# One TensorE row half for each of two heads in the first attention, gathers of four experts packed into three

## Chip, core and metric

The kernel runs on one core of a Trainium2 chip. The metric is the device time of one launch in microseconds. The core has TensorE (matmuls into PSUM), VectorE, ScalarE, GpSimd and SyncE (SP, which here only issues DMAs), and 16 DMA engines.

## What is computed

Two sequences of 1024 tokens with 256 features go through four blocks: a causal attention with rotary embedding (16 heads of 16 features), a layer norm with a ternary-weight projection, a causal attention with 16 heads of 128 features, and a mixture of 64 experts. Cut to the parts that the change touches:

```python
# first attention: x (2, 1024, 256), 16 heads of 16
q, k, v = proj(Wq), proj(Wk), proj(Wv)
q, k = rope(q), rope(k)
scores = where(causal, q @ k.T / 4, lowest)
attn = softmax(scores) @ v
y = attn @ Wo.T
# experts: 64, top 6 of 64 within the best 3 of 8 groups, capacity 96 rows each
slot = flat * C + min(pos, C - 1)
buf = zeros(E * C, H).at[slot].set(x[tok])
out = (silu(buf @ Wg.T) * (buf @ Wu.T)) @ Wd.T      # for each expert
y = sum(out[slot] * topk_w) + shared_expert(x)
```

All of it is float32. The kernel writes queries and keys of the attentions as sums of a high and a low f16 part.

## The kernel before

The stages follow each other with a barrier between them: norm, the projections of the first attention (`l0_qkv`), `l0_attention`, its output projection, the second layer, `norm`, `l1_attention` for each sequence, the router, `experts` and `combine`.

**`l0_attention`.** 32 heads (16 in each of two sequences) run one after the other; a pair of heads shares the value product. For each head GpSimd's `fetch` copies the parts of q and k into `qh` and `kh` (128 tokens by 8 blocks by 128 columns; 64 columns carry the four products of high and low parts, one more carries the maximum, the rest are zero). SP turns them with a DMA transpose (`turn`, lines 583 and 588). TensorE computes for each block of 128 queries the scores against all earlier keys (`max_scores`, "rows", line 624, the causal mask added by line 627), VectorE reduces them to the negated maximum, written into a column of `qh` (line 737), and SP turns `qh` once more (line 600). With that, TensorE computes for each block of keys the scores of all later queries less their maximum ("columns", line 682, mask 687), and ScalarE takes the exp into `pT` (line 725). The score banks are two deep for rows (`S1`) and two for columns (`ST`), each up to 1024 wide. TensorE alternates a column step and the row step that lies `EARLY` = 6 steps ahead. Within a pair's 16 steps `SESSIONS` puts ten rounds of value matmuls of the pair before (line 645: four matmuls into four column groups, f32) in four stretches; then ScalarE evacuates zT (line 714), TensorE turns it (658), VectorE divides (744, 751).

In the same block the weights of the second attention are split into f16 parts, 24 jobs: SP loads one (`w_load`, line 822; 16 jobs of 384 KB, then 8 of 256 KB), GpSimd splits it (`w_split`, lines 805, 811, 813), SP stores it (`w_store`, 827). There are two buffers for input and two for parts. GpSimd also issues 24 zero-fills of `choice_rows` (line 571), one a head. GpSimd's order in head m is `fetch(m)`, `fetch_values(m - 2)`, `w_split(m - 4)`, zero-fill; SP's is the turn of `qh` with the maxima of m, `turn(m + 2)`, `w_store(m - 3)`, `w_load(m - 1)`. Semaphores count: `w_in` for what is fetched, `t_in` and `tm_in` for what is turned, `m_ready` for maxima, `st_ready` and `s1_ready` for scores, `e_ready` for exps.

**`experts`.** The router leaves for each expert the list of its 96 tokens in `src` and of their destinations in `dst` (lines 1677 to 1685). GpSimd gathers the 96 rows of each expert (line 1742), 16 experts ahead; TensorE turns them, two experts at a time (`turn_pair`, 1779), VectorE copies them (1904). The expert's matmuls are `gu` (1793) and `down` (1802); ScalarE copies the result (1879) and GpSimd scatters it (1751). SP loads the experts' weights, 528 KB each, 16 ahead: the first 10 in the router, six more at the start of this block (lines 1722 to 1724), the others as buffers come free. At the start TensorE also finishes the shared expert's last four tiles (1412) and, between the first and the second expert, turns the weights of overflowing tokens (1823); VectorE and ScalarE take part (`overflow`, `turned_overflow`). `combine` then loads the rows of every token and adds them up.

## Time and profile before

| | |
|---|---|
| three runs | 1574.81, 1579.88, 1579.84 us; median 1579.84 |
| profiled execution | 1579.99 us, its span 1578.3 us |
| mean granted TensorE clock | 0.941 |
| first attention | about 96 to 398 us of the span |
| experts and combining | from about 1355 us to the end |

The span reaches from the first to the last instruction of the profiled execution; what lies around it makes up the rest of its time. Busy times are those of the profiler's records. A granted clock of 1.00 is 2.4 GHz, 0.50 is 1.2 GHz. "idle before <-X" names what ended an engine's idle time.

### The profile page before, as it was taken

The page shows a single profiled execution, that of the slowest core. Times are in us where ns is not written, and L with a number is a line of the kernel's source. Part 1 is how long each engine was busy: PE and PEld are TensorE (multiplying, and loading weights), DVE is VectorE, ACT ScalarE, POOL GpSimd, SP SyncE. Part 2 cuts the span into 40 slices and gives each one's busy share as a digit, 9 for nine tenths or more (in the row PEclk, how much of TensorE's full clock was granted, in tenths as well). Part 3 has the DMA queues.
Part 4 walks back from the last instruction along what each step waited for, and adds up shares of the span by engine and source line. Part 5 has one row for each costly group of instructions (what it writes and reads, how often), then busy time and mean ns, then how long its engine had stood idle before and what let it go on. Part 6 is the DMA issues. An engine that isn't in the chain of part 4 may idle for free. (4 is left out here: it accounts for less than half of the span.)

```text
span 1578.3 us, 36418 instructions
## 1 busy us (share of the span) xinstructions
PE 1407.0 (89%) x12869; PEld 985.8 (62%) x12869; DVE 1050.9 (67%) x2197; ACT 813.1 (52%) x1676; POOL 375.3 (24%) x796
## 2 busy tenths in 40 slices
PE   3848999998669999999979999999998798699977
PEld 2414555454555777777767677777777645599953
DVE  4766777775766888888841888888882368522229
ACT  1215656556216777777730787777781115333330
POOL 0344656430020111111120111111101000477730
PEclk9968999999869999999999999999999789799985
DMA  3027999972023755556540566556652340599948
GB/s 100 1 59 158 243 250 240 212 170 54 1 77 77 139 134 137 133 136 139 136 91 1 112 138 140 135 133 140 140 122 44 106 118 0 141 290 300 283 131 291
DMA packets 463402, 215.08 MB, mean 136 GB/s; under 512 B 412083, under 2 KB 434449, under 8 KB 463073
## 3 DMA queue, kind: packets, MB, share of 16 engines
q1 hardware_dynamic: 448992, 175.09, 46.9%
q0 software_dynamic: 12000, 36.90, 7.9%
q10 hardware_dynamic: 2336, 2.16, 0.4%
q8 instruction: 39, 0.64, 0.2%
q14 instruction: 35, 0.28, 0.1%
HBM read 81.97 MB, written 31.52 MB: 72 GB/s over the span
## 5 line engine op out<-in xcount | busy, mean ns | idle before, releaser
L1055 PE MATMUL bank<-a_pt,v_part 128*128 128x128 f16 x3456 | 234.2, 219 | 14.9 <-DMA a_pt<-a_ph 9.5
L737 DVE TENSOR_REDUCE a_qh<-bank 128x1 f16<-128x1024 f32 (+7 forms) x256 | 182.3, 755 | 86.5 <-PE bank L627 84.9
L1118 ACT ACTIVATE a_ph<-a_p,a_rinv 128x1024 f16<-128x1024 f32 (+7 forms) x256 | 198.6, 777 | 79.0 <-POOL a_rinv L997 76.0
L1055 PEld LDWEIGHTS bank<-a_pt,v_part 128*128 128x128 f16 x3456 | 207.7, 98 | 48.4 <-DMA a_pt<-a_ph 7.8
L1126 DVE TENSOR_REDUCE a_negm<-bank 128x1 f32<-128x1024 f32 (+7 forms) x256 | 191.8, 750 | 55.9 <-PE bank L1039 55.7
L1034 PE MATMUL bank<-a_k,a_q 128*128 128x512 f16 (+3 forms) x1152 | 228.6, 326 | 0.2
L725 ACT ACTIVATE a_p<-bank 128x1024 f32<-128x1024 f32 (+7 forms) x256 | 158.0, 650 | 129.8 <-PE bank L682 113.8
L1160 DVE SCALAR_TENSOR_TENSOR a_ph<-a_p,a_rinv,a_ph 128x1024 f16<-128x1024 f32 (+7 forms) x256 | 206.9, 808 | 1.7 <-ACT a_ph L1118 1.7
L1107 ACT ACTIVATE a_p<-bank,a_negm 128x1024 f32<-128x1024 f32 (+7 forms) x256 | 189.5, 740 | 21.6 <-DVE a_negm L1126 21.5
L997 POOL TENSOR_TENSOR a_rinv<-a_rinv,p_scale 128x1 f32<-128x1 f32 x256 | 49.0, 191 | 615.4 <-DVE a_rinv L1139 615.2
L906 PE MATMUL bank<-x_part,wsplit 128*128 128x512 f16 x768 | 187.3, 381 | 4.0 <-PEq L188 1.8
L624 PE MATMUL bank<-a_k,a_q 128*128 128x512 f16 (+3 forms) x384 | 109.5, 342 | 33.8 <-DMA a_k<-a_kh 19.4
L1034 PEld LDWEIGHTS bank<-a_k,a_q 128*128 128x128 f16 x1152 | 99.4, 98 | 60.6 <-ACT a_p L1107 1.2
L682 PE MATMUL bank<-a_qm,a_k 128*128 128x512 f16 (+3 forms) x384 | 113.0, 333 | 6.6 <-ACT a_p L725 5.2
L906 PEld LDWEIGHTS bank<-x_part,wsplit 128*128 128x128 f16 x768 | 70.1, 98 | 72.2 <-issue 5.6
L1742 POOL DMA_INDIRECT x_rows<-token_rows,src x64 | 63.1, 986 | 172.6 <-issue 170.2
L1793 PE MATMUL bank<-x_T,wgu 128*88 128x96 f32 x1024 | 96.4, 248 | 0.7 <-issue 0.7
L915 PE MATMUL bank<-wsplit,x_part 128*128 128x128 f16 x1536 | 95.9, 219 | 0.8 <-DVE a_k L941 0.5
L1793 PEld LDWEIGHTS bank<-x_T,wgu 128*88 128x88 f32 x1024 | 92.9, 158 | 4.5 <-issue 1.0
L915 PEld LDWEIGHTS bank<-wsplit,x_part 128*128 128x128 f16 x1536 | 88.2, 98 | 5.7 <-DVE a_k L941 2.1
L1911 DVE TENSOR_TENSOR x_h<-bank,x_sg 88x192 f32<-88x192 f32 x64 | 22.6, 354 | 94.8 <-ACT x_sg L1870 94.8
L1188 PE MATMUL bank<-wo_part,z_part 128*128 128x256 f16 x768 | 84.2, 273 | 1.7 <-PEq L966 1.7
(206 smaller groups left out, 2246.4 us busy)
## 6 DMA issues: line engine op xcount, KB each, us to landing
wgu<-in_wgu SPq DMA_DIRECT2D x64, 352.0 KB
choice_rows<-zero POOLq DMA_DIRECT2D x24, 512.0 KB, 5.2
c_rows<-choice_rows SPq DMA_DIRECT2D x16, 768.0 KB, 11.5
wsplit<-w_parts POOLq DMA_DIRECT2D x30, 384.0 KB, 3.9
wd<-in_wd SPq DMA_DIRECT2D x64, 176.0 KB
pw_in<-in_wqkv SPq DMA_DIRECT2D x16, 384.0 KB, 5.3
w_parts<-pw_part SPq DMA_DIRECT2D x16, 384.0 KB, 2.9
a_pt<-a_ph SPq DMA_TRANSPOSE x256, 3.0
```

Of the source, the lines that this page charges most:

```text
L682: ins = pe.matmul(ST[k % 2][:, c4 * 512:c4 * 512 + w_], kT[s][:, kb, :], queries[:, kb * P + c4 * 512:kb * P + c4 * 512 + w_], start=True, ...
L725: act.activation(pT[s][:, off[kb]:off[kb + 1]], ST[k % 2][:, 0:(BT - kb) * P], ACT.Exp).then_inc(e_ready, 1)
L737: dve.tensor_reduce(qh[s][:, i, MC:MC + 1], s1_place(t), AX.X, ALU.max, negate=True).then_inc(m_ready, 1)
L906: ins = pe.matmul(G_ps[k % 2], w[:, a, c_, (k // 2) * P:(k // 2 + 1) * P], g.xs[x_][:, c_, b * S + (k % 2) * 512:b * S + (k % 2 + 1) * 512 ...
L915: ins = pe.matmul(G_ps[k % 2][:, j * P:(j + 1) * P], g.xs[x_][:, c_, t * P:(t + 1) * P], w[:, a, c_, 2 * P:3 * P], start=(c_ == 0 and (a, ...
L1034: ins = eng.matmul(ps[:, c4 * 512:c4 * 512 + w_], qT[par][a][:, i * P:(i + 1) * P], kT[par][k_][:, c4 * 512:c4 * 512 + w_], start=(a, k_) ...
L1055: ins = eng.matmul(Z_ps[:, cols], g.vs[par][v_][:, k, :], turned[slot][:, a * blocks[j] + k, :], start=(k == 0 and (v_, a) == PARTS[0]), s ...
L1107: eng.activation(probs[j % NBUF][:, 0:w_], S_ps[j % 4][:, 0:w_], ACT.Exp, bias=negm[:, par, j:j + 1], accum_out=rsum[:, par, j:j + 1]).the ...
L1118: eng.activation(parts[slot][:, 0:w_], probs[slot][:, 0:w_], ACT.Copy, scale=rinv[:, p_, jj:jj + 1]).then_inc(p_hi, 1)
L1126: eng.tensor_reduce(negm[:, par, j:j + 1], S_ps[j % 4][:, 0:blocks[j] * P], AX.X, ALU.max, negate=True).then_inc(m_ready, 1)
L1160: eng.scalar_tensor_tensor(parts[slot][:, w_:2 * w_], probs[slot][:, 0:w_], rinv[:, p_, jj:jj + 1], parts[slot][:, 0:w_], ALU.mult, ALU.su ...
L1793: ins = pe.matmul(b_[:, m * C:(m + 1) * C], g.wgu[s][:, c_, m * MH:(m + 1) * MH], xeT[(s // 2) % 2][:, s % 2, c_, :], start=(c_ == 0), sto ...
```

## The change

In the first attention the two heads of a pair are packed into one set of tiles: head 0 in the first 64 rows of the turned tiles, head 1 in the other 64. Each head has 48 columns for three products (high by high, low by high, high by low; the product of the low parts is left out) and one for the maximum. Rows and columns are cut into pieces of at most 512 columns, 24 rows and 24 columns for a pair (`ROWS`, `COLS`, alternating between the heads); the banks are three deep on each side. In each step the row piece, which belongs to the other head than the column piece, is issued first, then the column piece, then the masks in halves of 64 rows (`swapped` holds identity and mask rolled by 64 rows). The maxima of blocks with two pieces are joined from `half`. The queries are copied a second time into `qhm` for the turn with the maxima, the keys are turned twice (`kT`, `kTb`). Value rounds come in five stretches of two. SP and GpSimd do one iteration for each pair, with two weight jobs in it.

In the experts three gathers of 128 rows bring four experts' 384 rows; `src` is packed for it by small matmuls with `c_shift` at the router's end; `turn_group` turns them in six transposes, and VectorE copies them in one instruction. SP's loads for experts 10 to 15 wait for the first turn. The overflow's turn is moved behind the experts' loop.

```diff
+                sp.dma_start(swapf[:, :, :], g.t["c_swapped"]).then_inc(s_c, 16)
...
-    MC = 4 * DH0
+    HP = P // 2
+    MC = 3 * DH0
-    w_in = [g.sem(f"a0_w{i}") for i in range(2)]
-    t_in = [g.sem(f"a0_turned{i}") for i in range(2)]
-    tm_in = [g.sem(f"a0_turned_max{i}") for i in range(2)]
-    v_in = g.sem("a0_v_in")
-    FETCH = 5
+    t_in, tb_in, tm_in = [g.sem(f"a0_turned{n}") for n in ("", "_keys", "_max")]
+    w_in, wm_in, v_in, c_ready = [g.sem(f"a0_{n}") for n in ("w", "w_max", "v_in", "max_column")]
+    FETCH = 4
     ROUNDS = 2 * CH + 2
-    SESSIONS = {1: (0, 1, 2), 3: (3, 4), 7: (5, 6), 9: (7, 8, 9)}
-    ZT_STEP, TURN_STEP, Z_STEP = 11, 13, 15
-    ORDER = (0, 7, 1, 6, 2, 5, 3, 4)
-    EARLY = 6
+    SESSIONS = {1: (0, 1), 5: (2, 3), 9: (4, 5), 13: (6, 7), 17: (8, 9)}
+    ZT_STEP, TURN_STEP, Z_STEP = 18, 20, 22
+    ROWS = ((6, 1), (6, 0), (4, 1), (5, 0), (5, 1), (7, 1), (2, 0), (7, 0), (0, 0), (3, 0), (1, 0), (4, 0))
+    COLS = ((0, 0), (7, 0), (0, 1), (6, 0), (1, 0), (5, 0), (2, 0), (3, 1), (3, 0), (2, 1), (4, 0), (1, 1))
+    NS = 2 * NC_
+    NB_ = 3
+    EARLY = 13
...
+        qhm = [g.sb(f"a0_qhm{i}", [P, BT, P], F16, c) for i in range(2)]
+        half = g.sb("a0_half", [P, 2, 2, BT // 2, 2], F32, c)
+        ST = [g.bank[0][:, 0, :], g.bank[0][:, 1, :], g.bank[1][:, 0, :]]
+        S1 = [g.bank[2][:, 0, :], g.bank[2][:, 1, :], g.bank[1][:, 1, :]]
...
+                def queries(dst, m, done):
+                    q = dst[m % 2].rearrange("p t (h c) -> p h t c", h=2)
+                    src = g.qk[:, 2 * m:2 * m + 2, :, 0, :]
+                    pool.tensor_copy(q[:, :, :, 0:2 * DH0], src).then_inc(done, 1)
+                    pool.tensor_copy(q[:, :, :, 2 * DH0:MC], src[:, :, :, 0:DH0]).then_inc(done, 1)
                 def fetch(m):
                     if m >= 2:
+                        pool.wait_ge(t_in, 32 * (m - 1))
+                        pool.wait_ge(tb_in, 16 * (m - 1))
+                    queries(qh, m, w_in)
+                    k = kh[m % 2].rearrange("p t (h c) -> p h t c", h=2)
+                    src = g.qk[:, 2 * m:2 * m + 2, :, 1, :]
+                    pool.tensor_copy(k[:, :, :, 0:DH0], src[:, :, :, 0:DH0]).then_inc(w_in, 1)
+                    pool.tensor_copy(k[:, :, :, DH0:MC], src).then_inc(w_in, 1)
+                def fetch_again(m):
+                    if m >= 2:
+                        pool.wait_ge(tm_in, 16 * (m - 1))
+                    queries(qhm, m, wm_in)
...
+                for m in range(2, NP):
                     fetch(m)
+                    fetch_again(m)
                     fetch_values(m - 2)
+                    for q in (2 * m - 4, 2 * m - 3):
+                        if q < WJOBS:
+                            w_split(pool, q)
+                        if q < ZD:
+                            pool.dma_start(zv[q], g.zero[:, :]).then_inc(g.s_zero, 16)
+                fetch_values(NP - 2)
+                fetch_values(NP - 1)
...
+                def turned(dst, src, m, done):
+                    sp.dma_start_transpose(dst[m % 2].rearrange("p (t n) -> p t n", n=P),
+                                           src[m % 2].rearrange("p t d -> p (t d)")).then_inc(done, 16)
                 def turn(m):
+                    sp.wait_ge(w_in, FETCH * (m + 1))
+                    if m >= 1:
+                        sp.wait_ge(t_in, 32 * m)
                     if m >= 2:
+                        sp.wait_ge(s1_ready, (m - 1) * NS)
+                    turned(kT, kh, m, t_in)
+                    turned(qT, qh, m, t_in)
+                def turn_keys(m):
+                    if m >= 1:
+                        sp.wait_ge(tb_in, 16 * m)
+                    if m >= 2:
+                        sp.wait_ge(st_ready, (m - 1) * NS)
+                    turned(kTb, kh, m, tb_in)
                 turn(0)
                 turn(1)
+                turn_keys(0)
                 w_load(sp, 0)
                 w_load(sp, 1)
+                for m in range(NP):
+                    sp.wait_ge(c_ready, 2 * m + 2)
+                    if m >= 1:
+                        sp.wait_ge(tm_in, 16 * m)
                     if m >= 2:
+                        sp.wait_ge(st_ready, (m - 1) * NS)
+                    turned(qmT, qhm, m, tm_in)
+                    if m + 2 < NP:
                         turn(m + 2)
+                    for q in (2 * m - 2, 2 * m - 1):
+                        if 0 <= q < WJOBS:
+                            w_store(sp, q)
+                    for q in (2 * m, 2 * m + 1):
+                        if 2 <= q < WJOBS:
+                            w_load(sp, q)
+                    if m + 1 < NP:
+                        turn_keys(m + 1)
...
+                def scores(col, row):
+                    if row is not None:
+                        t, m, par, at_start = row
+                        hr, i, k0, nr_ = row_piece(t)
+                        if t == 0:
+                            pe.wait_ge(t_in, m * 32 + 32)
+                        if not (at_start and t < NB_):
+                            pe.wait_ge(m_ready, m * NS + (t - NB_ + 1))
+                        at = slice(hr * HP, (hr + 1) * HP)
+                        rs = S1[t % NB_]
+                        r_diag = k0 + nr_ == i + 1
+                        ri = pe.matmul(rs[:, 0:nr_ * P], qT[par][at, i * P:(i + 1) * P],
+                                       kT[par][at, k0 * P:(k0 + nr_) * P], start=True, stop=not r_diag)
+                    if col is not None:
+                        k, m, par, at_start = col
+                        hc, kb, q0, nc_ = col_piece(k)
+                        if k == 0:
+                            pe.wait_ge(tm_in, m * 16 + 16)
+                            pe.wait_ge(tb_in, m * 16 + 16)
+                        if not (at_start and k < NB_):
+                            pe.wait_ge(e_ready, m * NS + (k - NB_ + 1))
+                        at = slice(hc * HP, (hc + 1) * HP)
+                        cs = ST[k % NB_]
+                        c_diag = q0 == kb
+                        ci = pe.matmul(cs[:, 0:nc_ * P], kTb[par][at, kb * P:(kb + 1) * P],
+                                       qmT[par][at, q0 * P:(q0 + nc_) * P], start=True, stop=not c_diag)
+                    for x in range(2):
+                        if row is not None and r_diag:
+                            ident, mask = halves(hr)[x]
+                            ri = pe.matmul(rs[:, (nr_ - 1) * P + x * HP:nr_ * P], ident, mask[:, x * HP:P],
+                                           start=False, stop=x == 1)
+                        if col is not None and c_diag:
+                            ident, mask = halves(hc)[x]
+                            ci = pe.matmul(cs[:, x * HP:(x + 1) * HP], mask, ident[:, x * HP:(x + 1) * HP],
+                                           start=False, stop=x == 1)
+                    if row is not None:
+                        ri.then_inc(s1_ready, 1)
+                    if col is not None:
+                        ci.then_inc(st_ready, 1)
...
+                    if i >= BT // 2:
+                        dve.tensor_reduce(half[:, par, h, i - BT // 2, k0 // 4:k0 // 4 + 1], S1[t % NB_][:, 0:n_ * P],
+                                          AX.X, ALU.max).then_inc(m_ready, 1)
+                    else:
+                        dve.tensor_reduce(qhm[par][:, i, h * HP + MC:h * HP + MC + 1], S1[t % NB_][:, 0:n_ * P],
+                                          AX.X, ALU.max, negate=True).then_inc(m_ready, 1)
+                    if t >= NS - 2:
+                        dve.wait_ge(m_ready, m * NS + (t + 1))
+                        dst = qhm[par][:, BT // 2:BT, h * HP + MC:h * HP + MC + 1].rearrange("p t o -> p (t o)")
+                        dve.tensor_reduce(dst, half[:, par, h, :, :], AX.X, ALU.max, negate=True).then_inc(c_ready, 1)
...
+            sp.wait_ge(s_t, 1)
...
+            def gather(n, j):
+                pool.indirect_dma_start(out=rows[n % NR][:, j, :], out_offset=None, in_=g.xrows,
+                                        in_offset=bass.IndirectOffsetOnAxis(ap=g.src[:, j, n:n + 1], axis=0),
+                                        bounds_check=T - 1, oob_is_err=False).then_inc(s_row[n % NR], 16)
+            for n in range(LOOK):
+                for j in range(NPK):
+                    gather(n, j)
...
+            def turn_group(n, q):
+                pe.wait_ge(s_row[q], n * (NPK * 16 // NR) + (NPK * 16 - NPK * 16 // NR * q))
+                if not (isinstance(n, int) and n == 0):
+                    pe.wait_ge(s_tc, n)
+                for c_ in range(DC):
+                    for j in range(NPK):
+                        ins = pe.transpose(g.bank[0][:, c_, j * P:(j + 1) * P],
+                                           rows[q][:, j, c_ * P:(c_ + 1) * P], g.identf[:, :])
...
+            pe.wait_ge(s_sf, 1)
+            for j in range(NPK):
+                for q, at in PACK[j]:
+                    ins = pe.matmul(packed[:, j, :], g.shift[:, at:at + P],
+                                    srcf.rearrange("p (e q) -> p e q", q=XG)[:, :, q],
+                                    start=(q == PACK[j][0][0]), stop=(q == PACK[j][-1][0]))
+            ins.then_inc(s_ix, 1)
...
-            walk(act, lambda p_num, s: None, silu, out_rows, turned_overflow)
+            walk(act, lambda p_num, s: None, silu, out_rows)
+            turned_overflow()
...
-            walk(dve, turned, product, lambda i, e, s: None, overflow)
+            walk(dve, turned, product, lambda i, e, s: None)
+            overflow()
```

## Rows read from the trace of the kernel before

**Rows 1.** Busy time by window, first attention: engines, granted clock, DMA share, GB/s.
```profile
160.00:200.00 40.00, 37.96 (x391) 20.36 (x393) 28.41 (x51) 24.18 (x40) 26.05 (x49) 1.00 1.03 246
...
320.00:360.00 40.00, 37.69 (x376) 20.33 (x368) 28.45 (x50) 24.61 (x41) 13.43 (x37) 1.00 0.73 160
```

**Rows 2.** Timeline of ScalarE: first and fourteenth evacuation of zT (start, duration).
```profile
151.13 0.60 ACT L714 ACTIVATE a_zt<-bank 128x512 f32<-128x512 f32 x1
...
373.14 0.60 ACT L714 ACTIVATE a_zt<-bank 128x512 f32<-128x512 f32 x1
```

**Rows 3.** Timeline of TensorE around a stretch of value matmuls.
```profile
242.84 0.22 PE L687 MATMUL bank<-identb,maskb 128*128 128x128 bf16 x1
242.89 0.33 PE L682 MATMUL bank<-a_qm,a_k 128*128 128x384 f16 x1
...
243.91 1.06 PE L645 MATMUL bank<-a_p,a_vh 128*17 128x256 f32 x16
244.90 0.39 PE L682 MATMUL bank<-a_qm,a_k 128*128 128x512 f16 x1
```

**Rows 4.** Busy time by window, start and middle of the experts.
```profile
1362.00:1366.00 4.00, 0.77 (x4) 0.34 (x2) 0.76 (x2) 0.00 (x0) 3.05 (x4) 0.97 1.05 276
1366.00:1370.00 4.00, 2.63 (x15) 2.37 (x16) 2.36 (x3) 0.00 (x0) 3.39 (x3) 0.50 0.81 247
...
1380.00:1420.00 40.00, 40.00 (x377) 36.16 (x376) 10.47 (x25) 12.03 (x34) 30.25 (x33) 1.00 0.98 289
```

**Rows 5.** Timeline of the experts' start.
```profile
1355.74 7.03 PE L1412 MATMUL bank<-sd,shared_h_late 128*128 128x256 f32 x24 [2.98 <-DVE x L1924]
...
1359.49 0.96 POOL L1742 DMA_INDIRECT x_rows<-token_rows,src  x1 [0.30 <-issue]
...
1366.67 0.90 PE L1779 MATMUL bank<-identf,x_rows 96*128 96x96 f32 x4 [3.90 <-DMA x_rows<-token_rows,src]
...
1374.25 1.49 PE L1793 MATMUL bank<-x_T,wgu 128*88 128x96 f32 x16
```

**Rows 6.** Groups by shape, first attention: count, busy us, mean ns.
```profile
L737 DVE TENSOR_REDUCE a_qh<-bank 128x1 f16<-128x512 f32 x32 | 21.9, 683 | 0.0
...
L813 POOL TENSOR_TENSOR pw_part<-pw_in,pw_part 128x512 f16<-128x512 f32 x8 | 9.2, 1151 | 0.7
...
L737 DVE TENSOR_REDUCE a_qh<-bank 128x1 f16<-128x128 f32 x32 | 9.1, 283 | 0.0
...
L811 POOL CAST pw_part<-pw_in 128x512 f16<-128x512 f32 x8 | 4.9, 614 | 23.0 <-DMA pw_in<-in_wo 23.0
```

**Rows 7.** Timeline of SP's issues and of GpSimd, one head.
```profile
245.00 0.61 POOL L805 TENSOR_TENSOR pw_in<-pw_in,pw_scale 128x256 f32<-128x256 f32 x1 [3.40 <-DMA pw_in<-in_wqkv]
...
246.16 1.33 SPq L588 DMA_TRANSPOSE a_k<-a_kh  x1
...
247.54 0.57 SPq L827 DMA_DIRECT2D w_parts<-pw_part  x1
...
248.16 0.59 POOL L571 DMA_DIRECT2D choice_rows<-zero  x1
248.16 0.46 SPq L822 DMA_DIRECT2D pw_in<-in_wqkv  x1
248.75 0.41 POOL L546 COPY a_qh<-qk_parts 128x256 f16<-128x256 f16 x1
```

**Rows 8.** DMA issues of 200 to 300 us: count, KB, median us to landing.
```profile
pw_in<-in_wqkv SPq DMA_DIRECT2D x7, 384.0 KB, 5.5
pw_in<-in_wo SPq DMA_DIRECT2D x5, 256.0 KB, 4.3
...
a_q<-a_qh SPq DMA_TRANSPOSE x12, 3.4
```

**Rows 9.** Timeline of the first attention's first score matmul and last exps.
```profile
105.82 0.61 PE L624 MATMUL bank<-a_k,a_q 128*128 128x512 f16 x1 [17.21 <-DMA a_k<-a_kh]
...
389.93 1.19 ACT L725 ACTIVATE a_p<-bank 128x640 f32<-128x640 f32 x2 [0.21 <-PE bank L682]
```

More of the change, by code:

```diff
@@ L696, in pair @@
-                def pair(which, p, n0, s0):
-                    for h in range(2):
-                        for k in range(BT):
-                            step(which, p, n0 + h, s0 + h, h, k)
-                            if which != "first":
-                                for r in SESSIONS.get(h * BT + k, ()):
-                                    value_round(pe, r, p - 1, n0 - 2, (s0 + 2) % 4)
+                    scores(None, (t, 1, 1, False))
+                def pair(which, p, par):
+                    for k in range(NS):
+                        ahead, t = s1_step(k)
+                        row = None if skipped(which, ahead) else (t, p + ahead, (par + ahead) % 2, False)
+                        scores((k, p, par, which == "first"), row)
+                        if k == TURN_STEP and which != "first":
+                            turn_z(pe, p - 1)
+                        if which != "first":
+                            for r in SESSIONS.get(k, ()):
+                                value_round(pe, r, p - 1, 1 - par)
@@ L1366 @@
 XG = 4
+NPK = XG * C // P
+PACK = [[(q, C + j * P - q * C) for q in range(XG) if q * C < (j + 1) * P and (q + 1) * C > j * P]
+        for j in range(NPK)]
+LOOK = 3
 XP = 10
```

319 lines of the change are left out of this document (124 added, 195 removed).

## The prediction

> **What bounds the kernel now.** I read the stretches of the first attention first (the table by window), because most of the diff is there. TensorE is busy 38 of 40 us, VectorE 28, ScalarE 24, GpSimd 13 to 26, and the DMA engines' share falls from 1.03 to 0.73 [rows 1]. Then the evacuations of zT, one for each pair of heads: 13 pitches in 222 us, 17.1 us a pair [rows 2]. The pitch is the same where the DMA share is 1.03 and where it is 0.73, so neither the DMA engines nor the splitting of the second attention's weights sets it: it is TensorE, with its waits for the two-deep score banks. One 128-column matmul with its weight load follows the other after 0.05 us, 16 value matmuls (two rounds) take 1.06 us from the first start to the last end, of which 0.2 are the last one's own pipeline, so 0.85, and 0.14 us more pass until the next score matmul [rows 3]. By hand, a pair of heads is 22,528 f16 columns (9.4 us at 2.4 GHz), 80 value matmuls (4.3), the turn of zT (0.6), so 14.3 of the 17.1 us. In the experts TensorE is busy all 40 of 40 us, with the DMA engines at 0.98 [rows 4]; ahead of them it waits 3.90 us for gathered rows [rows 5].
>
> **The first attention's new work on TensorE.** Each score piece now contracts over 64 rows, one head in each half of the array, and a row piece of one head is issued beside a column piece of the other. Counting both streams step by step and taking the longer of each step, I get 13,824 columns, 5.8 us a pair; 112 matmuls with weight loads at 0.05 us [rows 3] are 5.9. If the halves don't overlap, the 24,576 columns are 10.2 us. No row of before shows two row halves. The nearest shows column groups: 16 value matmuls of 256 f32 columns, which one after the other would take some 3 us, in 0.85 [rows 3]. I take the overlap. Then TensorE needs 5.9 + 4.3 + 0.6 + 5 gaps of 0.15 = 11.6 us.
> The Trainium skill (TensorE: Matmul & The Clock Gate, Part 3: Packing small matmuls) says that matmuls on distinct row groups run together; by it the 5.9 stands, and no row here shows it. A rule against the change is in TensorEngine Tiling (Array Packing), Tiling Modes: going from one tiling mode to another drains the engine. The 0.14 us gap behind a value stretch agrees; with ten such changes a pair instead of eight it is worth 0.3 us, within the gaps counted.
>
> **VectorE and ScalarE.** VectorE is busy 28.4/40 x 17.1 = 12.1 us a pair. The same 9,216 columns are now reduced in 24 pieces instead of 16; the fixed part of a reduction is 0.15 us (283 ns at 128 columns, 683 at 512 [rows 6]), half of it overlapped, so 8 x 0.07 = 0.6, and two small reductions over `half`, each behind a wait for its own predecessor, 0.5: 13.2 us. Five value stretches of 0.85 us leave it dry some 0.3 us each (three banks of at most 512 columns hold 1.4 to 1.7 us of its work, and the next piece comes 1.7 to 1.9 us later): 14.7 us a pair. The bounds are 13.2 and 17.1. ScalarE has 10.3 us and 8 more starts, about 11; it doesn't bind.
>
> **The loop that takes over: weights, GpSimd, SP.** This is the step on which I differ from the sum above. Before, a head's iteration of SP is qm turn, turn(m + 2), one store, one load, and GpSimd's is fetch(m), one split. A load goes out two iterations before the turn that its split delays, so the loop load, split, fetch, two turns, store spans two heads: 5.5 + 3.2 + 0.6 + 1.5 + 2.6 + 0.6 = 14 us in 17.1. After, an iteration is a pair: SP issues turn(m + 2), stores 2m - 2 and 2m - 1, then loads 2m and 2m + 1; GpSimd does fetch(m + 2) first and then splits 2m and 2m + 1. turn(m + 3) waits for w_in, thus for fetch(m + 3), which stands behind both splits of 2m and 2m + 1 on GpSimd; and the next two loads stand behind turn(m + 3) and both stores on SP. So everything is in one chain once a pair:
> zero-fill DMA 0.6, fetch with two copies of 512 and two of 256 elements 2.0 (256 take 0.41), two transposes issued 2.6, two stores 1.15, load to landing 5.5, split 3.15, zero-fill 0.6, split 3.15 [rows 7, 8] = **18.8 us**. For the eight `wo` jobs (four pairs) the landing is 4.3 [rows 8] and a split 1.15 + 0.61, with a gap 1.8 [rows 6]: 15.1 us.
> The nearest rows for each link are those of before, with the same SP and GpSimd operations; unknown are only the 512-element copies (between 0.41 and 0.82) and the landing beside two stores and a second load (5.2 to 6.5). That gives 18.2 to 20.5 for the loop.
> It is above 14.7, so after the slack is gone (turn(m) is some 7 us ahead at first) pairs go at the loop's pace, and TensorE waits about 4 us a pair for `a0_turned` at step 11, the first row piece of the pair after next.
>
> **The attention's timeline.** First score matmul at 105.8 as now [rows 9]. 37 row pieces come before the first column, at VectorE's 0.6 us: columns from 128, and c_ready for pair 1 eleven steps later, at 134. From there to fetch(4): qm and two turns 3.9, stores 1.15, landing 5.5, splits and zero-fills 7.5, fetch 2.0: 154. Six loops of 18.8 and four of 15.1 bring fetch(14) to 327.3, and its turn lands 4.7 later (one issue, and 3.4 to landing [rows 8]), at 332, step 11 of pair 12. Then two pairs at 14.7, 13 steps with columns alone 7.0, the last pair 12.5 (TensorE: 12,288 columns in one stream 5.1, value matmuls 4.3, turn 0.6, gaps and waits 2.5): 381. Before, the last exp ends at 391.1 [rows 9]. **-10.2 us.** The final ten value rounds are as they were.
>
> **The experts.** The gathers are 48 of 128 rows instead of 64 of 96, the turns six of 128 columns instead of eight of 96, the same 768 columns; GpSimd and VectorE aren't the bound there. So the pace (377 matmuls in 40 us [rows 4], 22 an expert, 2.34 us) stays: 0 (bounds -3 and +3). The start changes. Now TensorE finishes the late shared rows at 1362.8, gets its rows at 1366.67 (the fourth gather, issued at 1359.49, lands 7.1 us later beside 3.2 MB of weights), and with the turned overflow in between the second expert's matmuls start at 1374.25 [rows 5]. After, three gathers suffice and SP's 12 weight loads wait for the first turn; I take the landing at 1362.8 or earlier (between 1360.5 and 1365.3). Turn 0.7, a copy of 768 columns 1.0, first expert 1.5, waits 0.3, packing at the router's end 0.6 later (one VectorE copy behind 12 small matmuls): the second expert at 1366.9 + 0.6 = 1367.5. **-6.7 us** (bounds -4 and -8). The overflow's turn now lies where TensorE and VectorE wait for the combining rows, over 10 us, and needs 6: hidden. The 12 loads are 8 us late; the first of these experts is wanted some 20 us later: nothing.
> The load of `c_swapped` ahead of x costs one issue, **+0.5**. The extra casts and `c_shift` lie behind x and the norm: 0.
> Sum: 1579.99 (the profiled execution, 1578.3 of span and 1.7 around it; the median of three is 1579.84) - 10.2 - 6.7 + 0.5 = **1564 us**.
>
> **Rivals.**
> A, the loop does not bind, because loads, fetch or issue are quicker together than I add up or more work is ahead than I count. For it: the loop of today has 3 us to spare and never shows in the pitch. Against: the order of the two programs. Attention then 128 + 13 + 13.5 x 14.7 + 19.5 = 358, -33: **1541 us**. Chance 0.14.
> B, the change doesn't do what it says: the row halves run one after the other. Then a pair is 17.9 us of TensorE; hidden under 18.8 six times, +2.8 in four pairs and +3.2 in two, some 2 at both ends, +20: **1584 us**. Chance 0.12, for only column groups are shown.
> C, the loop is longer, 20 to 20.5, its landing slowed by two stores and a second load: +10 to +15, **1577 us**. For it: stores and loads of this stage have never stood this close together. Chance 0.08.
> D, the clock. After 3.9 us of waiting for the rows of the experts the granted clock was 0.50, the 1.2 GHz level, against 0.97 in the stretch ahead [rows 4]; the wait of 4 us a pair at step 11 is as long. At 1.2 GHz a pair is 2 x 10.2 + 1 = 21 us. A clock low for half of the pair gives 17.6 us and stays hidden under 18.8; low for over about 70% of it, it is the new bound, and low throughout +2.4 in six pairs and +6 in four: **1603 us**, slower. Chance 0.05.
> The forecast itself 0.61, with its own range 1556 to 1573.
>
> **Numbers.** 0.5% is 7.9 us, about what a measurement here can tell. Faster: 0.53 of the forecast's 0.61, all of A, 0.01 of C = 0.68. Slower: B 0.04, C 0.02, D 0.05 = 0.11. The same: 0.21. The range reaches from A to B, 1540 to 1586.
>
> **What would show it.** Right: evacuations of zT 18 to 20 us apart for six pairs, then 15, then less than 15; the first row piece of each pair waiting for the DMA of `a0_k` or `a0_q`; SP waiting in the turn for GpSimd's copies; GpSimd waiting for pw_in. Overlap: row and column matmuls starting within 0.05 us with a step no longer than its wider piece. Wrong if the pitch is 14 to 15 from pair 2 on (A), if steps with two 512-column pieces last over 0.45 us at full clock (B), or if the stretches show a clock near 0.5 (D). In the experts the first turn should come at once behind the shared rows.

## The result and the profile after

The kernel after takes 1561.28 us (median of four runs, 1559.74 to 1562.85), the kernel before 1579.86 beside it: ratio 0.988 with a 95% interval of 0.9856 to 0.9904. The profiled execution took 1561.47 us, its span is 1559.4, 18.9 less than before.

First the pace of the first attention, by the page's most plain mark, ScalarE's evacuation of zT once a pair (line 787). Its starts are 148.49, 163.63, 179.04, 199.09, 214.59, 233.54, 251.92, 268.34, 283.49, then 14.9 to 15.0 apart up to 328.25, and 342.75, 356.84, 369.87, 377.24. Before it was 17.0 from pair to pair (once 17.7, the last two less) and ended at 395.40: the attention is 18.2 us shorter. Busy time by window (as [rows 1]):

```profile
160.00:200.00 40.00, 32.34 (x460) 17.05 (x457) 30.82 (x74) 25.54 (x60) 24.45 (x35) 0.91 0.74 200
...
320.00:360.00 40.00, 34.54 (x519) 18.00 (x511) 30.77 (x79) 30.10 (x72) 3.96 (x9) 1.00 0.38 75
```

TensorE has 32 us of work in 40 where it had 38; no engine is busy all the time. TensorE's timeline around a stretch of value matmuls (as [rows 3]; 729 is a row piece, 744 a column piece, 696 the values):

```profile
172.05 0.39 PE L729 MATMUL bank<-a_k,a_q 64*128 64x512 f16 x1
172.13 0.38 PE L744 MATMUL bank<-a_qm,a_kb 64*128 64x512 f16 x1
...
172.50 1.06 PE L696 MATMUL bank<-a_p,a_vh 128*17 128x256 f32 x16
173.50 0.33 PE L729 MATMUL bank<-a_k,a_q 64*128 64x384 f16 x1
173.50 0.33 PE L744 MATMUL bank<-a_qm,a_kb 64*128 64x384 f16 x1
```

Row and column piece of these steps start 0 to 0.08 us apart: the two halves of the array work at once. A step of two 512-column pieces takes 0.22 us up to its masks (171.53 to 171.75). What sets the pitch stands on SP's and GpSimd's timelines (as [rows 7]):

```profile
149.81 0.62 POOL L585 COPY a_qh<-qk_parts 128x512 f16<-128x512 f16 x1
...
151.67 1.23 SPq L633 DMA_TRANSPOSE a_k<-a_kh  x1
152.96 1.33 SPq L633 DMA_TRANSPOSE a_q<-a_qh  x1
154.34 1.07 SPq L909 DMA_DIRECT2D w_parts<-pw_part  x2
155.45 1.78 SPq L904 DMA_DIRECT2D pw_in<-in_wqkv  x2
...
160.59 0.61 POOL L887 TENSOR_TENSOR pw_in<-pw_in,pw_scale 128x256 f32<-128x256 f32 x1 [7.70 <-DMA pw_in<-in_wqkv]
...
168.14 0.62 POOL L585 COPY a_qh<-qk_parts 128x512 f16<-128x512 f16 x1
...
170.01 1.23 SPq L633 DMA_TRANSPOSE a_k<-a_kh  x1
```

From turn to turn 18.34 us: two turns 2.67, stores 1.11, load to first split 5.14, two splits and two zero-fills 7.55, copies 1.87. The turn of pair 4 (pairs are numbered from 0) starts at 151.67, that of pair 10 at 259.33: six loops of 17.9 us on average. The other links are the same in all six to 0.02 us; what varies is the landing, 4.49 to 5.14 us, 4.75 in the mean. TensorE gets the end of it, and its clock too (its timeline, and windows of 2 us):

```profile
192.36 0.50 PE L729 MATMUL bank<-a_k,a_q 64*128 64x384 f16 x1 [3.07 <-DMA a_q<-a_qh]
```

```profile
188.00:190.00 2.00, 1.29 (x22) 0.46 (x17) 1.70 (x5) 1.11 (x3) 0.98 (x3) 1.00 0.57 105
190.00:192.00 2.00, 0.00 (x0) 0.00 (x0) 0.10 (x1) 0.00 (x0) 0.00 (x0) 0.84 1.07 246
192.00:194.00 2.00, 1.64 (x18) 0.98 (x21) 0.83 (x2) 0.89 (x2) 0.00 (x0) 0.50 1.09 324
194.00:196.00 2.00, 2.00 (x23) 0.67 (x24) 0.92 (x2) 0.68 (x2) 0.00 (x0) 0.50 0.94 332
196.00:198.00 2.00, 2.00 (x24) 0.98 (x24) 1.67 (x4) 1.61 (x4) 1.84 (x3) 0.50 1.19 235
198.00:200.00 2.00, 1.52 (x28) 0.93 (x21) 1.22 (x4) 1.20 (x5) 1.98 (x3) 0.95 0.33 73
```

Behind the wait of 3.07 us the granted clock is 0.50, the 1.2 GHz level, for almost 7 us. That makes this pitch 20.05 us, but the next is 15.50 and the two together are again two loops: the slow clock is hidden behind the loop.

The experts' start (as [rows 5]); the first turn of gathered rows (line 1885) now comes straight behind the late shared rows (1502), and the clock of 1352 to 1356 is 1.00 where it was 0.50 behind the old wait:

```profile
1344.13 7.60 PE L1502 MATMUL bank<-sd,shared_h_late 128*128 128x256 f32 x24 [1.52 <-DVE x L2029]
1351.57 0.82 PE L1885 MATMUL bank<-identf,x_rows 128*128 128x128 f32 x6
1353.48 2.85 PE L1899 MATMUL bank<-x_T,wgu 128*88 128x96 f32 x32 [1.10 <-DVE x L2029]
```

Where the 18.9 us come from: attention -18.2; the blocks up to the second attention another -1.9; the second attention, in which nothing was changed, gives back 7.0; the experts' start, from the router's copy of `dst` (1354.02 before, 1340.81 after) to the second expert's first matmul (1374.25 and 1354.85), -6.2; the rest is +0.3, and rounding.

### The profile page after: what moved, and what is told of

Same layout as the page of the kernel before. It is cut to its first block and busy times, and to the rows that moved or that the text cites. A ratio compares the mean times of both kernels' runs of the same rounds, so it can differ in the third digit from the quotient of the medians.

```text
span 1559.4 us, 37733 instructions
## 1 busy us (share of the span) xinstructions
PE 1373.0 (88%) x13361; PEld 969.1 (62%) x13361; DVE 1061.9 (68%) x2343; ACT 821.2 (53%) x1804; POOL 354.4 (23%) x698
## 5 line engine op out<-in xcount | busy, mean ns | idle before, releaser
L1116 PE MATMUL bank<-a_k,a_q 128*128 128x512 f16 (+3 forms) x1152 | 228.7, 326 | 0.2
L797 ACT ACTIVATE a_p<-bank 128x512 f32<-128x512 f32 (+3 forms) x384 | 166.3, 492 | 103.4 <-PE bank L753 84.8
L812 DVE TENSOR_REDUCE a_half<-bank 128x1 f32<-128x512 f32 (+3 forms) x256 | 137.4, 583 | 38.7 <-PE bank L749 36.2
L729 PE MATMUL bank<-a_k,a_q 64*128 64x512 f16 (+3 forms) x384 | 117.8, 360 | 50.2 <-DMA a_q<-a_qh 26.7
L744 PE MATMUL bank<-a_qm,a_kb 64*128 64x512 f16 (+3 forms) x384 | 109.4, 343 | 1.8 <-ACT a_p L797 1.6
L729 PEld LDWEIGHTS bank<-a_k,a_q 64*128 64x128 f16 x384 | 34.5, 96 | 101.3 <-DVE a_half L812 44.4
L1849 POOL DMA_INDIRECT x_rows<-token_rows,src x48 | 49.1, 1024 | 169.2 <-POOLq L1591 154.9
```

What stands on the lines that cost most here:

```text
L729: ri = pe.matmul(rs[:, 0:nr_ * P], qT[par][at, i * P:(i + 1) * P], kT[par][at, k0 * P:(k0 + nr_) * P], start=True, stop=not r_diag)
L797: act.activation(pT[2 * par + h][:, at:at + n_ * P], ST[k % NB_][:, 0:n_ * P], ACT.Exp).then_inc(e_ready, 1)
L812: dve.tensor_reduce(half[:, par, h, i - BT // 2, k0 // 4:k0 // 4 + 1], S1[t % NB_][:, 0:n_ * P], AX.X, ALU.max).then_inc(m_ready, 1)
L1116: ins = eng.matmul(ps[:, c4 * 512:c4 * 512 + w_], qT[par][a][:, i * P:(i + 1) * P], kT[par][k_][:, c4 * 512:c4 * 512 + w_], start=(a, k_) ...
```

## The experiments

Ten kernels ran. Times are medians, the ratio is to the kernel before.

**1. Stores and loads ahead of the turns.** SP's order alone.

```diff
                     turned(qmT, qhm, m, tm_in)
-                    if m + 2 < NP:
-                        turn(m + 2)
                     for q in (2 * m - 2, 2 * m - 1):
                         if 0 <= q < WJOBS:
                             w_store(sp, q)
                     for q in (2 * m, 2 * m + 1):
                         if 2 <= q < WJOBS:
                             w_load(sp, q)
+                    if m + 2 < NP:
+                        turn(m + 2)
```

> Changed against the kernel after: SP issues the two stores and the two loads of a pair ahead of turn(m + 2), not behind it. My theory: the loop of 17.9 us a pair in the kernel after is the once-a-pair chain fetch, two turns, stores, loads, landing, two splits. With this order fetch and turn hang beside it, and stores 1.15, landing 5.0, splits and a zero-fill 6.9 make 13.1 to 13.6 us, under the 14.9 us that pairs take at the end of the attention, where no weights are moved. So all pitches of zT come to 14.9 to 15.5 us, the wait of TensorE for the row turn (26.7 us in seven places) goes, and the kernel takes about 1547 us, 14 less than the 1561 of the kernel after. Rival (the longer pitch of the pairs with weight jobs comes from TensorE, VectorE or the transfers being slower beside 0.75 of DMA share): the pitch stays at 17 to 18 us and the time at 1561 +- 2.

1547.05 us, ratio 0.978 [0.9751, 0.9809], 14.2 us below the kernel after; the last evacuation of zT comes 14.3 us earlier, at 362.98. Every pitch from the second to the tenth pair is 14.88 to 15.15 us, no wait of TensorE is over 1 us from 140 to 345, and no window of 2 us there has a clock below 0.9. SP's and GpSimd's timelines:

```profile
206.96 1.05 SPq L909 DMA_DIRECT2D w_parts<-pw_part  x2
208.05 1.71 SPq L904 DMA_DIRECT2D pw_in<-in_wqkv  x2
209.87 2.08 SPq L633 DMA_TRANSPOSE a_k<-a_kh  x1
...
214.45 0.61 POOL L887 TENSOR_TENSOR pw_in<-pw_in,pw_scale 128x256 f32<-128x256 f32 x1 [4.27 <-DMA pw_in<-in_wqkv]
...
221.41 0.59 POOL L626 DMA_DIRECT2D choice_rows<-zero  x1
...
221.93 1.05 SPq L909 DMA_DIRECT2D w_parts<-pw_part  x2
```

GpSimd still waits for the load, but 4.27 us, not 7.70: turns and copies now lie beside the landing. The chain was the bound, and the order of two issues made it. The rival is out: the DMA share rises to 0.93 in 160 to 200 and the pitch falls. What is left of the chain is longer than the 13.1 to 13.6 us expected, since the load lands later beside the turns: stores 1.09, load to first split 6.40, splits and a fill 6.96 make 14.5 us, only 0.4 under the pitch.

**2. Row and column piece in the same half.**

```diff
-    EARLY = 13
+    EARLY = 12
```

> Changed against the kernel after: EARLY 12 instead of 13, so that in each step the row piece and the column piece belong to the same head, and so lie in the same half of the rows of TensorE; all else is as it was. My theory (pieces in different halves run together and are worth 4 us of TensorE a pair): matmuls of a step start one behind the other, the pitch at the end of the attention, without weight jobs, goes from 14.9 to 17.5 to 18.5 us, and the pairs with weight jobs from 17.9 to 18 to 19; the kernel takes 1575 to 1585 us. Rival (VectorE sets the 14.9 us, and the overlap of the halves is worth little in time): pitches 14.9 to 15.5 at the end, the time 1561 +- 3.

1582.67 us, ratio 1.0027 [1.0012, 1.0043]. The pitch is 17.33 to 17.38 us from the second pair to the eleventh, with weight jobs and without: TensorE binds everywhere. It is busy 36.8 us in each 40 (180 to 340), 15.9 a pair. The loop of the turns still takes 18.0 us on average (154.06 to 262.03, six loops); the pitch doesn't show it, since the turns start some way ahead. TensorE's timeline:

```profile
337.07 0.39 PE L729 MATMUL bank<-a_k,a_q 64*128 64x512 f16 x1
337.30 0.38 PE L744 MATMUL bank<-a_qm,a_kb 64*128 64x512 f16 x1
```

0.23 us from row to column where the kernel after has 0 to 0.08; a step of two 512-column pieces takes 0.45 us instead of 0.22. The overlap is worth 2.4 us of pitch and 21 us of the whole; without it the change gains nothing. (The edit also shortens the lead of the rows by one step; that was not tried by itself.)

**3. Both zero-fills ahead of both splits.**

```diff
                     for q in (2 * m - 4, 2 * m - 3):
-                        if q < WJOBS:
-                            w_split(pool, q)
                         if q < ZD:
                             pool.dma_start(zv[q], g.zero[:, :]).then_inc(g.s_zero, 16)
+                    for q in (2 * m - 4, 2 * m - 3):
+                        if q < WJOBS:
+                            w_split(pool, q)
```

> Changed against the kernel after: GpSimd issues a pair's two zero-fills ahead of its two splits instead of one behind each, where it waits for the load anyway. My theory (a single chain once a pair through GpSimd and SP): 2 x 0.6 us leave the chain, the loop goes from 17.9 to 16.7 us in six pairs and from 14.6 to some 14.6 (there TensorE and VectorE bind), the kernel takes about 1554 us. Rival (the chain is not what binds, or the landing only fills the place of what leaves it): 1561 +- 2 and pitches of 17.9.

1601.72 us, ratio 1.0148 [1.0128, 1.0167]: 40 us slower than the kernel after, where I expected 7 less. Both theories miss. The loop is 21.2 us:

```profile
173.41 1.23 SPq L634 DMA_TRANSPOSE a_k<-a_kh  x1
174.70 1.34 SPq L634 DMA_TRANSPOSE a_q<-a_qh  x1
176.09 3.33 SPq L910 DMA_DIRECT2D w_parts<-pw_part  x2
179.47 2.59 SPq L905 DMA_DIRECT2D pw_in<-in_wqkv  x2
```

```profile
174.57 1.13 POOL L624 DMA_DIRECT2D choice_rows<-zero  x2
186.36 0.61 POOL L888 TENSOR_TENSOR pw_in<-pw_in,pw_scale 128x256 f32<-128x256 f32 x1 [10.67 <-DMA pw_in<-in_wqkv]
```

The fills' issue did leave the chain (1.2 us), but their transfers, 1 MB, now start 1.5 us ahead of SP's stores. The stores take 3.33 us to issue, not 1.07, the loads 2.59, not 1.78, and land in 6.6 us instead of 4.9 (medians of 200 to 260). From turn to first split it is 12.95 us where it was 8.92. In the kernel after a fill lands 2.9 us after its issue, before the next stores go out; here it takes 5.7 and is still under way beside them. TensorE waits 3.9 to 5.3 us in each of seven pairs, and the clock falls to 0.50 with each. In the prediction's sum a fill was its 0.6 us on GpSimd and no more. Experiments 5 and 6 ask what it is.

**4. The experts' part alone** (everything but the first attention as after; the attention as before).

> The experts' part of the change alone: everything as in the kernel after, but the first attention as it was before. My theory: the experts' part is worth 6 us, all at the start of the experts, and the first attention of the kernel after the rest, less what the granted clock takes back in the second attention: the kernel takes about 1574 us, and in the second attention the clock does not drop in the last heads (nothing in it has changed). Rivals: the clock's drop there comes with any of this change's parts or at random (then 1574 to 1581 with the drop in it); the gain of 6 us belongs to the earlier arrival at the experts, not to the packing (then 1580).

1575.56 us, ratio 0.9969 [0.9953, 0.9986]. The experts start as after: 17.5 us from the packing to the second turn (17.2 in the kernel after), first turn at once behind the late shared rows. So the 6 us belong to the experts' edits and not to the earlier arrival. The total shows only 3.4, since the unchanged second attention is 2.4 us longer by its clock: my expectation that the clock would not drop is wrong, and its rival (1574 to 1581, with the drop) holds.

**5. Zero-fills behind the loop.**

```diff
-                        if q < ZD:
-                            pool.dma_start(zv[q], g.zero[:, :]).then_inc(g.s_zero, 16)
                 fetch_values(NP - 2)
                 fetch_values(NP - 1)
+                for q in range(ZD):
+                    pool.dma_start(zv[q], g.zero[:, :]).then_inc(g.s_zero, 16)
```

> Changed against the kernel after: GpSimd issues the 24 zero-fills behind its last fetch of the first attention, not in its loop. What is disputed since the kernel with both fills ahead of the splits took 21.4 us a pair where the kernel after takes 17.9: my sum counts a fill as its 0.6 us of issue on GpSimd. Theory 1 (a fill costs its issue alone, the 21.4 has another cause): 1.2 us leave the loop, 16.7 us a pair, some 1554 us. Theory 2 (its 512 KB of transfer stand ahead of SP's stores and loads as well): the loop falls below the 14.9 us that TensorE and VectorE want, pitches of 15 to 15.5, and the kernel takes 1547 to 1550 us, if the fills' transfers at the end collide with nothing.

1565.89 us, ratio 0.9912 [0.9879, 0.9944]. In the attention theory 1 holds: the turns of pairs 4 to 10 start at 150.34 and 250.92, a loop of 16.8 us where it was 17.9, so a fill costs its 0.6 us of issue and no more. The load lands as it did (4.74 us from load to first split in the mean, 4.75 in the kernel after). Neither theory's total holds. The attention ends 8.6 us earlier (368.69), and then:

```profile
348.21 12.90 POOL L628 DMA_DIRECT2D choice_rows<-zero  x24
```

```profile
385.44 2.87 ACT L1370 ACTIVATE z<-z_by_head 128x256 f32<-128x256 f32 x9 [16.15 <-PEq L568]
```

The next block starts only at 385.44, 16.8 us behind the last evacuation instead of 2.6. That is when the 12.6 MB of fills are through (the DMA engines' share over 370 to 386 is 0.76, in the kernel after it is 0.00 there); that the block waits for them is argued from this coincidence. The 8.6 us won came back one block later, and 5.6 more.

**6. Both fills between the two splits.**

```diff
                         if q < WJOBS:
                             w_split(pool, q)
-                        if q < ZD:
-                            pool.dma_start(zv[q], g.zero[:, :]).then_inc(g.s_zero, 16)
+                        if q % 2 == 0:
+                            for z in (q, q + 1):
+                                if z < ZD:
+                                    pool.dma_start(zv[z], g.zero[:, :]).then_inc(g.s_zero, 16)
```

> Changed against the kernel after: both zero-fills of a pair are issued between its two splits (the second one stands behind the second split in the kernel after, just ahead of the fetch, the turns and the stores). The number of instructions in the chain is the same. Theory 1 (issue alone counts): the loop stays at 17.9 us, the kernel at 1561 +- 2. Theory 2 (the transfer counts, by when it runs): both fills' transfers now run beside the second split, not beside the stores and loads; the loop is 16.5 to 17.5 us and the kernel takes 1554 to 1559 us.

1562.5 us, ratio 0.9873 [0.9826, 0.992]: theory 1 (1561 +- 2). The turns of pairs 4 to 10 start at 150.84 and 257.70, a loop of 17.8 us (17.9 in the kernel after; loops 17.48 to 18.52, so 0.1 tells nothing). With 3 and 5, all over the same six loops (experiment 3: 152.45 to 279.93, 21.2 us each), and taken from the 16.8 us without fills: both fills between the splits cost 1.0 us, one there and one behind the second split 1.2, which is their issue alone; both just ahead of the stores and loads, with their issue no longer in the chain, 4.5. So the transfer of a fill is free in both places beside or behind a split, and costs some 2.2 us where SP's stores and loads stand right behind it.

**7. Four stretches of value rounds, on experiment 1.**

```diff
-    SESSIONS = {1: (0, 1), 5: (2, 3), 9: (4, 5), 13: (6, 7), 17: (8, 9)}
+    SESSIONS = {1: (0, 1, 2), 7: (3, 4, 5), 13: (6, 7), 17: (8, 9)}
```

> Changed against the first experiment's kernel (stores and loads ahead of the turns, 1547 us, 14.9 us a pair throughout): ten value rounds in four stretches of 3, 3, 2 and 2 behind steps 1, 7, 13 and 17, not in five of 2. My theory (a stretch of two rounds leaves VectorE dry some 0.3 us, one of three leaves it dry 0.7 to 0.8, since three banks hold no more work than 1.4 to 1.7 us): one stretch less and two longer ones give -0.3 + 2 x 0.4 = +0.3 to +0.6 us a pair, 1552 to 1557 us. Rival (VectorE's own 13.2 us and its waits do not depend on the stretches' length): 14.9 us a pair and 1547 +- 2.

1551.97 us, ratio 0.9823 [0.978, 0.9867]; pitches 15.31 to 15.45, +0.4 a pair. As expected, three rounds at a time leave VectorE dry longer: from 180 to 300 us it is idle for 18.0 us, in experiment 1 for 14.0.

**8. Column piece first, on experiment 1.** The two blocks of `scores` that wait and issue are exchanged.

```diff
                 def scores(col, row):
-                    if row is not None:
-                        t, m, par, at_start = row
...
                     if col is not None:
                         k, m, par, at_start = col
...
+                    if row is not None:
+                        t, m, par, at_start = row
...
                     for x in range(2):
```

> Changed against the first experiment's kernel (1547 us, 14.9 us a pair): in each step the column piece is issued ahead of the row piece. The pieces still lie in different halves. My theory (VectorE, with 13.2 us of work in a pitch of 14.9, binds through the row pieces, and the column of a step starts at most 0.08 us behind the row): a row piece comes later by that start, and by the wait for ScalarE's exp when this is the later one: +0.1 to +0.5 us a pair, 1549 to 1555 us. Rival (the order within a step is worth nothing because both start together): 1547 +- 2.

1543.21 us, ratio 0.9766 [0.9723, 0.9808], the lowest median of all, but within the spread of experiment 1 (1540.65 to 1549.81). What is clear is the pitch: it falls to 14.72 to 14.77 from the second pair on. My theory has the wrong sign, and the rival (no effect) is off as well. The groups by line of 180 to 300 us, first of experiment 1, then of this kernel (line 730 is its column piece):

```profile
L729 PE MATMUL bank<-a_k,a_q 64*128 64x512 f16 x192 | 54.4, 328 | 11.9 <-DVE a_half L812 10.6 <-DVE a_qhm L815 0.3
L744 PE MATMUL bank<-a_qm,a_kb 64*128 64x512 f16 x192 | 53.4, 329 | 0.0
```

```profile
L730 PE MATMUL bank<-a_qm,a_kb 64*128 64x512 f16 x197 | 56.6, 328 | 4.4 <-ACT a_p L797 2.8
L744 PE MATMUL bank<-a_k,a_q 64*128 64x512 f16 x197 | 54.7, 330 | 4.0 <-DVE a_half L812 2.2
```

With the row first, each wait for VectorE's bank also holds back a column whose bank is free. With the column first it is issued inside that wait: 11.9 us of idle time become 8.4. The attention ends 1.4 us earlier (last evacuation 361.56, not 362.98); the rest of the 3.8 us between the medians lies behind it, in code that is the same in both, and isn't shown to come from this edit.

**9. No wait ahead of the weight loads, on experiment 8.**

```diff
-            sp.wait_ge(s_t, 1)
             for e in range(XP, XB):
```

> Changed against the kernel with the column piece first (1543 us): SP's loads of the weights of experts 10 to 15 don't wait for the first turn of gathered rows, they start with the block as before the change. My theory (the wait takes the weights' transfers from beside the first gathers): the third gather, issued 2.7 us behind the first, lands 6 to 7 us later instead of 4.0, the first turn comes 1.5 to 2.5 us behind the last late shared matmul instead of at once, and the granted clock may fall to 0.50 behind that wait, as before the change: 2 to 4 us longer up to the second expert, 1545 to 1547 us. Rival (three gathers instead of four are enough by themselves, the 7.6 us of late shared matmuls cover them even beside the weights): the turn at once, 1543 +- 1.5.

1550.75 us, ratio 0.9816 [0.9773, 0.9858].

```profile
1326.88 7.60 PE L1502 MATMUL bank<-sd,shared_h_late 128*128 128x256 f32 x24 [1.52 <-DVE x L2028]
1336.92 0.88 PE L1884 MATMUL bank<-identf,x_rows 128*128 128x128 f32 x6 [2.44 <-DMA x_rows<-token_rows,src]
1338.90 5.39 PE L1898 MATMUL bank<-x_T,wgu 128*88 128x96 f32 x32 [1.10 <-issue]
```

The first nine gathers land in 6.8 us in the median (4.0 in the kernel after, where the first three, for which the turn waits, take 2.8 in the median), the wait of 2.44 us is back, and behind it the clock is 0.76 and 0.50 (1336 to 1344). From the late shared rows to the second turn it is 18.5 us, in experiment 8 12.9: +5.6, above the 2 to 4 expected, since the low clock stretches the first experts' 2.85 us to 5.39. Three gathers in place of four would not have been enough: from the `dst` copy to the ninth expert's matmuls it is 36.24 us here, 30.66 in the kernel after and 36.54 before, so the wait on SP is what almost all of the experts' start hangs on.

**10. Ten stretches of one round, on experiment 8.**

```diff
-    SESSIONS = {1: (0, 1), 5: (2, 3), 9: (4, 5), 13: (6, 7), 17: (8, 9)}
+    SESSIONS = {1: (0,), 3: (1,), 5: (2,), 7: (3,), 9: (4,), 11: (5,), 13: (6,), 15: (7,), 16: (8,), 17: (9,)}
```

> Changed against the kernel with the column piece first (1543 us, 14.74 us a pair): ten stretches of one value round (behind steps 1, 3, 5, 7, 9, 11, 13, 15, 16, 17) instead of five of two. My theory (VectorE has some 13.1 us of work a pair and runs dry only in a stretch of two or more, 0.3 us each; a stretch of one takes TensorE some 0.5 us and stays within what three banks hold): a pitch of 13.6 to 14.3 us, 1532 to 1540 us. Rival (every change from score matmuls over 64 rows to value matmuls over 128 costs TensorE 0.1 to 0.15 us, and the steps behind one-round stretches are no wider): 14.7 to 15.3 us a pair, 1543 to 1551 us.

1549.95 us, ratio 0.9798 [0.9768, 0.9829]. The pitch is 15.13 to 15.18: the rival.

```profile
236.21 0.63 PE L696 MATMUL bank<-a_p,a_vh 128*17 128x256 f32 x8
236.77 0.39 PE L730 MATMUL bank<-a_qm,a_kb 64*128 64x512 f16 x1
```

A stretch of one round takes 0.56 us up to the next score, one of two 0.99 (235.80 to 236.79 in experiment 1). Ten of one are 5.6 us, five of two 4.95: 0.65 more for TensorE, of which 0.4 reach the pitch. VectorE doesn't gain by it: its idle time from 180 to 300 us is 16.5 us, in experiment 8 13.3. With experiment 7, two rounds a stretch are the best of the three.

## Why the prediction was right, and where it was off

**The sum.** 1564 predicted, 1561.28 measured. The closeness is partly luck: the attention gave 8 us more than forecast, and 7 came back in a stage that I took as unchanged.

**The overlap** (5.9 us of scores a pair, rival B 17.9 a pair and 1584): the halves do run together, and with them in one half the kernel is rival B almost to the number, 17.35 a pair and 1582.67. Rival B's terms (10.2, 4.3, 0.6 and the gaps) add up to 15.9, though; the other 2.0 us have no source in the prediction. In experiment 2 TensorE is busy 15.9 us a pair and idle 1.4. The Trainium skill's rule (TensorE: Matmul & The Clock Gate, Part 3: Packing small matmuls), that distinct row groups run together, agrees with the starts 0 to 0.08 us apart. The Trainium skill's rule on the drain between modes (TensorEngine Tiling (Array Packing), Tiling Modes) agrees with 2 x 0.56 - 0.99 = 0.13 us for one more stretch of values, against the 0.14 I took for one [rows 3]. A stretch is two changes of mode, so the two changes that the kernel after has more cost 0.13 us a pair, not the 0.3 forecast for them.

**The pitch of TensorE and VectorE** (14.7, with VectorE at 13.2): 14.9 measured, at the end of the kernel after and throughout experiment 1, where VectorE is busy 35.02 of 40 us, 13.1 a pair. TensorE was put too low: 11.6 forecast, 104.57 us busy in the 120 of 180 to 300 in experiment 1, so 13.0 a pair (the profiler's busy time counts more than the hand sum: before, it is 16.2 where that sum gave 14.3). With both engines at some 13 of 14.9 us it isn't shown that VectorE alone sets the pitch: experiment 7, with longer stretches, costs VectorE idle time and 0.4 us of pitch; experiment 10, with more work for TensorE, costs 0.4 as well.

**The loop.** Its place and its links were right, and experiment 1 shows it to be the bound. The size was off: 18.8 forecast, 17.9 measured. Nearly all of it is the landing, 4.75 us in the mean (5.5 taken); the copies are 1.87 (2.0). What TensorE sees of it was forecast too evenly: pitches of 18 to 20 us for six pairs and a wait of 4 us in each, measured 15.4 to 20.05 (three of them over 18) and waits for `a_q` of 3.1 us at most, 10.6 us in all from 140 to 345. The four `wo` loops should have bound at 15.1, but the prediction's own terms for them add up to 14.85; they came every 14.6 us on average, and it was TensorE and VectorE that bound there. The zero-fill at 0.6 was right where it stands (0.6 by experiment 5), and would have been wrong by 2 us in another place.

**The timeline** is the step that was mis-sized: -10.2 forecast, -18.2 measured. The first column piece came at 124.40, not 128 (the row pieces ahead of it went faster than 0.6 us each), fetch(4) 2.3 us earlier than 154, the six loops gave 5.1 (107.7 us, not 112.8), the four others 1.9 (58.5, not 60.4), and the end took back 1.3 or so. An error of 0.9 us in a chain that repeats six times is over a quarter of what the attention gained, and the slip in the `wo` loops made another 1.0 of the four loops' 1.9.

**The experts** (-6.7, bounds -4 to -8): -6.2. The terms (1362.8 + 0.7 + 1.0 + 1.5 + 0.3 + 0.6) add up to 1366.9, not to 1367.5, so they say -7.3. The packing was put too low: the late shared rows start 3.32 us behind the `dst` copy, 1.72 before, so 1.6 us and not 0.6. The first turn at once behind the shared rows, the pace unchanged (9.41 us from turn to turn, four experts), the overflow's turn hidden (its 3.24 us at 1505.09, while the first combining rows let TensorE wait until 1514.20). The load ahead of x: +0.3, not +0.5.

**Left out of the sum**: the clock in the second attention, +7.0 us in this execution (below).

**Rival A** (the loop does not bind, 1541) did not happen, but is what experiments 1 and 8 make of the kernel: 1547 and 1543. **C** (a landing slowed by stores and a second load) did not happen: 5.14 at most. Experiment 3 shows its mechanism, with fills in place of stores: 40 us. **D** (the clock falls behind the wait) happened in three of the pairs with weight jobs, for 3 to 7 us each, and stayed hidden under the loop as that rival's condition says (over 70% of a pair would have shown).

## What to carry to other kernels

When two iterations are merged into one, write the queues' order out again for the merged iteration: what was spread over two heads became one chain of 18 us here, and moving two issues gave 14 us, nearly as much as the whole change. Here it paid to issue the load first, which has the longest way to go. A DMA's price can be more than its issue: ask what is issued on any queue while it is under way. Where two streams share an in-order engine, try first the one that waits less: it was worth 0.2 us a pair here.

## What the runs showed of the hardware that was not expected

**The same code with a different clock.** From the first to the last evacuation of `z_part` the second attention's code is the same in all these kernels. It took 687.4 us before, 694.4 after, and between 689.7 and 694.2 in the ten experiments. All of the difference between before and after lies in the last heads of the two calls and behind them (3.4 us at the end of the first, 3.6 at the end of the second), where TensorE waits up to 3.5 us at a time for `a_pt` (in the first call's last 20 us 2.71 us at the longest before and 2.91 after). Windows of 4 us there, before, then after:

```profile
809.00:813.00 4.00, 1.85 (x27) 1.51 (x27) 0.69 (x1) 0.60 (x1) 0.00 (x0) 1.00 0.31 70
813.00:817.00 4.00, 3.30 (x31) 2.97 (x32) 0.35 (x2) 0.00 (x0) 0.00 (x0) 1.00 0.00 0
```

```profile
791.00:795.00 4.00, 2.18 (x27) 1.91 (x27) 0.72 (x2) 0.60 (x1) 0.00 (x0) 0.64 0.11 24
795.00:799.00 4.00, 3.59 (x18) 2.56 (x19) 0.32 (x2) 0.00 (x0) 0.00 (x0) 0.51 0.00 0
```

The same 27 matmuls of a head run at 2.4 GHz in one execution and mostly at 1.2 in the other, and the output projection behind them too. What decides it stays open. At the end of the first call all eleven other kernels lose 2.4 to 4.8 us against before, experiment 4 with the experts' part alone among them, so it may belong to the change and not to chance; but there is one profile of each. At the end of the second call only the kernel after and experiments 3 and 6 lose some 3 us more. The kernel before by itself ranges from 1573.21 us at a mean clock of 0.945 to 1587.19 at 0.935. A gain of less than 7 us ahead of such a stage can be hidden by it in one execution.

**A clock that fell without a long wait.** In experiment 10 two pitches were 16.65 and 16.40 us. Ahead of the first TensorE idled no longer than 0.47 us at a time, yet:

```profile
228.00:230.00 2.00, 1.22 (x19) 0.49 (x19) 2.00 (x8) 1.15 (x3) 0.80 (x2) 1.00 1.08 359
230.00:232.00 2.00, 2.00 (x20) 0.71 (x21) 0.98 (x4) 0.53 (x2) 1.92 (x2) 0.59 1.27 269
```

Longer single waits of 0.55 to 0.57 us in the same attention were followed by no such fall. In experiment 8, with the same work in other stretches, the second to the eleventh pitch are 14.72 to 14.77.

**Fills that hold up another queue's issue.** In experiment 3 SP's two stores took 3.33 us to issue behind 1 MB of GpSimd's fills, against 1.07 without them in front, and load to first split took 6.6 to 7.4 us against 4.5 to 5.1. That SP's issues wait for the fills' transfers is read from these times; the mechanism behind it is not shown.
